# Inverting 64 unit triangles per tile: four block levels of two products each, or five doubling stages

## What is computed

```
sab = S @ kk_t
S   = S * exp(w_t) + sab (x) b_t + v_t (x) k_t
y_t = S @ r_t
```

## Time and profile before

| | |
|---|---|
| median of three runs | 6516.54 us |
| the profiled execution | 6509.57 us, span 6507.4 us |
| TensorE busy | 5869.2 us (90%) |
| VectorE busy | 3906.5 us (60%) |
| ScalarE busy | 1874.9 us (29%) |
| GpSimd busy | 937.7 us (14%) |
| mean granted TensorE clock | 0.973 |

### The profile page before, as it was taken

How to read it: one execution, slowest core, us unless ns; L and a number is a source line. 1 busy time by engine, 2 the same in 40 slices (tenths; PEclk the granted TensorE clock), 3 DMA queues, 4 the chain that set the end, 5 groups by cost and what they waited for, 6 DMA issues and landing times. The chain is left out here.

```text
span 6507.4 us, 293913 instructions
## 1 busy us (share of the span) xinstructions
PE 5869.2 (90%) x135752; PEld 4180.8 (64%) x135752; DVE 3906.5 (60%) x9323; ACT 1874.9 (29%) x3531; POOL 937.7 (14%) x900
## 2 busy tenths in 40 slices
PE   6888988998988888898888988987499999999999
PEld 5777777777777777777777777776244444444443
DVE  5777777777777777777777777775523323322300
ACT  3333333333333333333333333332000000000000
POOL 0111111111111111111111111110202202220210
PEclk9999999999999999999999999998699999999999
DMA  1000000000000000000000000000211211121120
GB/s 57 21 18 17 23 17 18 23 17 17 23 17 17 23 18 17 22 19 17 23 18 17 24 17 17 24 15 14 90 46 66 73 65 60 60 92 46 66 71 13
DMA packets 108833, 214.34 MB, mean 33 GB/s; under 512 B 25424, under 2 KB 26704, under 8 KB 107088
## 3 DMA queue, kind: packets, MB, share of 16 engines
q1 hardware_dynamic: 92240, 144.98, 7.6%
q0 software_dynamic: 15360, 50.48, 2.3%
HBM read 144.67 MB, written 50.72 MB: 30 GB/s over the span
## 5 line engine op out<-in xcount | busy, mean ns | idle before, releaser
L377 DVE COPY_PREDICATED time_raw<-time_known,w_bank 128x96 f32<-128x96 int32 (+6 forms) x3072 | 823.5, 274 | 240.3 <-PE w_bank L874 151.9
L1661 PE MATMUL moe_bank<-moe_w,moe_hidden 128*128 128x512 f32 x2048 | 928.7, 596 | 0.0
L1648 PE MATMUL moe_bank<-moe_hT,moe_w 128*128 128x512 f32 x2048 | 924.8, 594 | 0.8 <-DVE moe_hT L1548 0.8
L1648 PEld LDWEIGHTS moe_bank<-moe_hT,moe_w 128*128 128x128 f32 x2048 | 386.8, 191 | 472.3 <-issue 471.1
L1661 PEld LDWEIGHTS moe_bank<-moe_w,moe_hidden 128*128 128x128 f32 x2048 | 379.4, 190 | 429.5 <-issue 428.1
L1569 ACT ACTIVATE moe_hidden<-moe_bank,moe_b 128x512 f32<-128x512 f32 x256 | 175.9, 687 | 1628.2 <-PE moe_bank L1648 1522.9
L860 PE MATMUL w_bank<-time_invT,time_part 32*32 32x32 f32 x32768 | 418.7, 196 | 141.1 <-issue 88.2
L860 PEld LDWEIGHTS w_bank<-time_invT,time_part 32*32 32x32 f32 x32768 | 372.4, 107 | 201.3 <-issue 138.5
L849 PE MATMUL w_bank<-time_inv,time_ub 32*32 32x32 f32 x32768 | 412.6, 196 | 72.9 <-issue 38.7
L849 PEld LDWEIGHTS w_bank<-time_inv,time_ub 32*32 32x32 f32 x32768 | 355.0, 107 | 190.4 <-issue 149.9
L802 POOL TENSOR_TENSOR time_tail<-time_tail,time_lp 128x512 f32<-128x512 f32 x64 | 75.4, 1178 | 2777.8 <-ACT time_lp L732 2682.9
(11 more groups left out here) (225 smaller groups left out, 9716.9 us busy)
## 6 DMA issues: line engine op xcount, KB each, us to landing
moe_w<-in_w SPq DMA_DIRECT2D x64, 1024.0 KB, 7.2
mid_xn<-time_xn_rows SPq DMA_DIRECT2D x128, 129.0 KB, 2.7
time_x_rows<-in_x SPq DMA_DIRECT2D x128, 128.0 KB, 2.9
time_base<-in_x SPq DMA_DIRECT2D x128, 128.0 KB, 3.2
mid_acc<-time_mixed SPq DMA_DIRECT2D x128, 128.0 KB, 2.7
mid_scores<-time_rated SPq DMA_DIRECT2D x128, 2.0 KB, 1.7
moe_b<-in_b SPq DMA_DIRECT2D x8, 256.0 KB
time_receptance<-in_w_receptance SPq DMA_DIRECT2D x1, 1024.0 KB, 4.9
```

The costliest lines, as they stand in the source:

```text
L377: e.copy_predicated(by_raw[:, "uy".index(q), n0:n1, :, 0:8 * j + 8], known[:, "uy".index(q), :, :, mine].to_broadcast([P, n1 - n0, 2, 8 * ...
L1648: got = e.matmul(up[now % 3][:, :], w1[:, g * F + k * P:g * F + (k + 1) * P], hT[x % 2][:, g * CAP + half * HALF:g * CAP + (half + 1) * HA ...
L1661: got = e.matmul(down[t][:, :], hidden[now % 4][:, t * P:(t + 1) * P], tile(w2, k), start=k == 0, stop=k == FC - 1)
```

## The change

Five stages with k = 1, 2, 4, 8, 16 take the place of the four levels. `ew` holds, side by side for each unit, 32 columns E and 32 columns W. E is one factor of a Newton-like doubling and W is the inverse so far. A stage multiplies a turned factor by both (64 moving columns); the first stage needs E alone and the last needs W alone (32 columns each). Results go to both PSUM banks 6 and 7. ScalarE copies them back to `ew`, VectorE turns the E half into `grow`, and GpSimd computes `2I - grow` for the next stage. There is no `P` and `Q` pair: each stage is one run of 64 products. In the TensorE order S1, S2, S4 and S8 stand where P0, P1, P2 and P3 stood, the places of Q0, Q1 and Q2 are empty, and S16 stands where Q3 stood. GpSimd's fill with the identity and the masks `levels` are gone; GpSimd makes the first E of the next tile from `ub` (`B.e1`).

```diff
@@ on_tensor
-            def P_of(lev, half):
-                    ...
-                        e.wait_ge(dve.sem, dve[f"C.I{lev - 1}"])
-                        mm = e.matmul(BANK[f"P{lev}"][head(h), blk(n)], got["ub"][head(h), blk(n)], got["inv"][head(h), blk(n)],
-            def Q_of(lev, half):
-                    e.wait_ge(act.sem, act[f"C.P{lev}"])
-                        mm = e.matmul(BANK[f"Q{lev}"][head(h), blk(n)], part[head(h), blk(n)], got["invT"][head(h), blk(n)],
+            def inverse_stage(k, half):
+                if half == 0:
+                    clear(e, f"S{k}")
+                    clear(e, f"S{k}+")
+                    if k == 1:
++                        ...
+                        e.wait_ge(pool.old, pool.ago("B.e1"))
+                    else:
+                        e.wait_ge(pool.sem, pool[f"C.b{k // 2}"])
+                taken = {1: slice(0, N), 16: slice(N, 2 * N)}.get(k, slice(0, 2 * N))
+                by = raw_of(0) if k == 1 else grow
+                for i in range(half * HALF_U // 2, (half + 1) * HALF_U // 2):
+                    for n in (i, i + HALF_U):
+                        ...
+                            mm = e.matmul(both_banks[to, n * 2 * N + taken.start:n * 2 * N + taken.stop], by[rows, blk(n)],
+                                          got["ew"][rows, n * 2 * N + taken.start:n * 2 * N + taken.stop],
@@ on_vector
-            def invert(lev):
-                e.wait_ge(pe.sem, pe[f"C.Q{lev}"])
-                e.copy_predicated(chunks(got["invT"]), level(lev + 1, U), chunks(BANK[f"Q{lev}"])).then_inc(
-                if lev < 3:
-                    e.transpose(col(got["inv"]), col(got["invT"])).then_inc(dve.sem, dve.step(f"C.I{lev}"))
+            def turn_rest(k):
+                e.wait_ge(act.sem, act[f"C.S{k}"])
+                e.transpose(chunks(grow), rest_of(got["ew"])).then_inc(dve.sem, dve.step(f"C.t{k}"))
...
                 mask_scores("u", 4)
                 mask_scores("u", 5)
+            if Cs:
+                turn_rest(8)
...
-                e.transpose(col(out["ub"]), raw_of(0)).then_inc(dve.sem, dve.step("B.ub"))
-            if Cs:
-                invert(3)
-                e.copy_predicated(chunks(out["invT"]), level(0, U), chunks(out["ub"])).then_inc(
-                e.transpose(col(out["inv"]), col(out["invT"])).then_inc(dve.sem, dve.step("B.inv"))
+                e.transpose(sum_of(out["ew"]), chunks(raw_of(0))).then_inc(dve.sem, dve.step("B.ub"))
@@ on_scalar
+            def inverse_of(k):
+                e.wait_ge(pe.sem, pe[f"C.S{k}"])
+                if k == 1:
+                    e.copy(rest_of(got["ew"]), rest_of(both_banks)).then_inc(act.sem, act.step("C.S1"))
+                elif k == 16:
+                    e.copy(chunks(invT), sum_of(both_banks)).then_inc(act.sem, act.step("C.S16"))
+                else:
+                    e.copy(col(got["ew"]), inv_bank).then_inc(act.sem, act.step(f"C.S{k}"))
@@ on_gpsimd
-                e.tensor_copy(chunks(out["invT"]), wt["eye"][:, :].rearrange("p (o t) -> p o t", o=1).to_broadcast(
+            def grow_of(k):
+                e.wait_ge(dve.sem, dve[f"C.t{k}"])
+                e.tensor_tensor(chunks(grow), every_unit(wt["eye2"]), chunks(grow), ALU.subtract).then_inc(
...
                 queries_of("u", 0, kkn)
+            if Cs:
+                grow_of(1)
...
                 faded_of(0)
+                grow_of(2)
+                grow_of(4)
+                grow_of(8)
+                e.wait_ge(dve.sem, dve["B.ub"])
+                e.tensor_tensor(rest_of(out["ew"]), every_unit(wt["eye2"]), sum_of(out["ew"]), ALU.subtract).then_inc(
@@ on_tensor, the order around the last stage
             if Bs:
                 score("u", 4)
                 score("u", 5)
             if Cs:
-                Q_of(3, 0)
+                inverse_stage(16, 0)
             if A:
                 for name in ("mk", "aaa", "ma"):
                     ...
             if Cs:
-                Q_of(3, 1)
+                inverse_stage(16, 1)
```

More of the change, by code:

```diff
@@ L89 @@
 KEYS = 8 * (1 + 2 + 3 + 4)
+TURN = 0
+HALF_U = U // 2
+STAGES = (1, 2, 4, 8, 16)
 UNITS = [(0, 3), (3, 6), (6, 9), (9, 12), (12, 14), (14, 16)]
@@ L172, in time_mix @@
         handed = [{n: sb(f"{n}_{i}", width) for n, width in (
-            ("ub", G * P), ("inv", G * P), ("invT", G * P), ("vT", G * P), ("decay_end", U), ("shrink", U))} for i in range(2)]
+            ("ew", 2 * G * P), ("vT", G * P), ("decay_end", U), ("shrink", U))} for i in range(2)]
         for i in range(2):
@@ L180, in time_mix @@
         yTs = [sb(f"yT{i}") for i in range(2)]
-        part, rhs, corr = sb("part"), sb("rhs", SU * N), sb("corr", SU * N)
+        grow, invT, rhs, corr = sb("grow"), sb("invT"), sb("rhs", SU * N), sb("corr", SU * N)
         state, faded, grown = sb("state", SU * N), sb("faded", SU * N), sb("grown", SU * N)
@@ L256, in time_mix @@
         ACT_STEPS = (
-            "A.carried A.x B.ek3 C.P0 A.mix B.ek012 D.squares B.eq D.lnv N.lnv D.rstd N.rstd B.v C.P1 A.hid_g A.hid_w A.hid_a "
-            "D.affine0 D.affine1 D.affine2 D.affine3 A.hid_kkk A.hid_mk C.P2 A.exp_z A.tail A.k C.P3 A.tna A.tnma "
-            "A.thmk A.sq N.xn B.e0 B.decay_end B.shrink C.u0 A.lp A.lns N.ln2 A.rs N.rs2 C.y0 C.u1 A.decayed A.r C.y1").split()
+            "A.carried A.x B.ek3 C.S1 A.mix B.ek012 D.squares B.eq D.lnv N.lnv D.rstd N.rstd B.v C.S2 A.hid_g A.hid_w A.hid_a "
+            "D.affine0 D.affine1 D.affine2 D.affine3 A.hid_kkk A.hid_mk C.S4 A.exp_z A.tail A.k C.S8 A.tna A.tnma "
+            "A.thmk C.S16 A.sq N.xn B.e0 B.decay_end B.shrink C.u0 A.lp A.lns N.ln2 A.rs N.rs2 C.y0 C.u1 A.decayed A.r C.y1").split()
         POOL_STEPS = (
-            "B.rk B.eye B.qu B.qy C.faded0 A.lt B.us C.faded1 B.ys").split()
+            "B.rk B.qu C.b1 B.qy C.faded0 C.b2 C.b4 C.b8 B.e1 A.lt B.us C.faded1 B.ys").split()
         PE_STEPS = (
-            "A.x D.centre C.P0 A.mix A.scored C.Q0 D.var A.delta D.gate B.value C.P1 B.bonus A.gate1 A.low_wa A.delta3 B.u0 C.Q1 "
-            "B.u1 A.low_k C.P2 B.u2 C.Q2 A.key B.u3 A.decay C.P3 B.u4 B.u5 A.low2 C.Q3 B.y0 B.y1 A.sums C.z0 B.y2 "
+            "A.x D.centre C.S1 A.mix A.scored D.var A.delta D.gate B.value C.S2 B.bonus A.gate1 A.low_wa A.delta3 B.u0 "
+            "B.u1 A.low_k C.S4 B.u2 A.key B.u3 A.decay C.S8 B.u4 B.u5 A.low2 C.S16 B.y0 B.y1 A.sums C.z0 B.y2 "
             "B.y3 C.u0 C.y0 D.out B.y5 B.y4 C.z1 C.u1 A.recept C.y1").split()
@@ L459, in on_vector @@
             if Cs:
-                invert(0)
+                turn_rest(1)
             if A:
@@ L845, in P_of @@
                     else:
-                        e.wait_ge(dve.sem, dve[f"C.I{lev - 1}"])
-                for n in range(half * U // 2, (half + 1) * U // 2):
-                    for h in range(HG):
-                        mm = e.matmul(BANK[f"P{lev}"][head(h), blk(n)], got["ub"][head(h), blk(n)], got["inv"][head(h), blk(n)],
-                                      start=True, stop=True, skip_group_check=True)
-                if half:
-                    mm.then_inc(pe.sem, pe.step(f"C.P{lev}"))
@@ L854, in Q_of @@
-            def Q_of(lev, half):
-                if half == 0:
-                    clear(e, f"Q{lev}")
-                    e.wait_ge(act.sem, act[f"C.P{lev}"])
-                for n in range(half * U // 2, (half + 1) * U // 2):
-                    for h in range(HG):
-                        mm = e.matmul(BANK[f"Q{lev}"][head(h), blk(n)], part[head(h), blk(n)], got["invT"][head(h), blk(n)],
-                                      start=True, stop=True, skip_group_check=True)
-                if half:
-                    mm.then_inc(pe.sem, pe.step(f"C.Q{lev}"))
+                        e.wait_ge(pool.sem, pool[f"C.b{k // 2}"])
@@ new lines, in inverse_stage @@
+                taken = {1: slice(0, N), 16: slice(N, 2 * N)}.get(k, slice(0, 2 * N))
+                by = raw_of(0) if k == 1 else grow
+                for i in range(half * HALF_U // 2, (half + 1) * HALF_U // 2):
+                    for n in (i, i + HALF_U):
+                        turned_in = TURN * (n // HALF_U) * (k in (4, 16))
+                        turned_out = TURN * (n // HALF_U) * (k in (2, 8))
+                        for h in range(HG):
+                            rows, to = head((h + turned_in) % HG), head((h + turned_out) % HG)
+                            mm = e.matmul(both_banks[to, n * 2 * N + taken.start:n * 2 * N + taken.stop], by[rows, blk(n)],
+                                          got["ew"][rows, n * 2 * N + taken.start:n * 2 * N + taken.stop],
+                                          start=True, stop=True, skip_group_check=True)
@@ L1171, in time_mix_inputs @@
     t = row % N
-    same = lambda size: t // size == i // size
-    upper = {h: same(2 * h) & (t // h == i // h - 1) for h in (1, 2, 4, 8, 16)}
     f32 = lambda a: np.ascontiguousarray(a.astype(np.float32))
@@ L1199, in time_mix_inputs @@
```

(1 more changed line is left out.)

100 lines of the change are left out of this document (43 added, 57 removed), and 8 rows, old and new, of the table DVE_STEPS.

## The result

The changed kernel takes 6733.8 us (median of four runs, 6726.7 to 6740.1), against 6517.0 for the kernel before (median of four runs beside it): a ratio of 1.034 (95% interval 1.032 to 1.036), 217 us slower. The forecast was 6595 us with a range of 6430 to 6680, so the direction was right and the size lies outside the range.

What follows compares the result with a forecast made beforehand. TensorE was taken to set the pace at 69.8 us a turn; 68.9 us of path plus 2.3 of low clock gave 71.2, +1.4 a turn over some 62 turns, +85 us: 6595 us, range 6430 to 6680.

Steps and rivals of the forecast that it cites:

- the path's sum: Eight links through one turn, stalls included: 68.9 us a turn at full clock without issue gaps.
- the issue gaps: TensorE waits the profile does not explain, 1.9 us a turn before two lines; forecast to be gone after the change.
- the five stalls: TensorE waits before `var` 1.5, u1 2.0, S4 1.2, S8 0.6 and S16 4.0 us; 9.3 us in sum.
- case D: Rival: issue gaps stay, clock falls at three places; 73.9 us a turn at worst, half the excess 6680 us; chance 0.13.
- link 4: Path from u2 through masked copies, transpose, hop, subtraction, hop to S8 at 2033.9; TensorE stalls 0.6 us.
- The clock's term: Lower TensorE clock behind stalls: 1.6 stretches a turn at 1.43 us, 2.3 us; mean clock about 0.96.
- A: Rival: same path, but stalls do not lower the clock; turn 68.9 to 69.2 us, about 6460 us; chance 0.16.
- B: Rival: stalls shorter than added up, most saved work arrives; at best 67.6 us a turn, 6375 us; chance 0.10.
- C: Rival: stalls come, clock stays as in the kernel before; 70.1 us a turn, 6530 us; chance 0.15.
- the 2.0 us of work: TensorE half runs fall from 10.9 to 8.9 us a turn; forecast that the stalls eat this saving.

Runs made afterwards that it cites:

- v4: Changed kernel with stages, VectorE turns and ScalarE copies reordered, no product added or left out: 6248.3 us, 0.961 of the kernel before.
- The control: Kernel before, four levels and products untouched, with `gate` behind delta3 and the squares and copy of P0 first on ScalarE: 6481.0 us, ratio 0.992.

## Why the prediction was wrong

*Right.* The direction; the work on TensorE (16 half runs to 10, 1.03 us for 64 columns); every link of the path from the start of the turn to S4 within 0.35 us; S16 5.1 us behind u4 (4.94); and that the clock falls where the stalls are. What the forecast named as tests came out so: 3.7, 1.0, 1.8 and 1.4 us of stall before S16, S4, u1 and `var` where 4, 1.2, 2 and 1.5 were forecast, and the waits on issue down from 3.4 to 0.8 us a turn. The exception is the size of the clock's fall: 0.92 where 0.96 was forecast.

*The step that failed is the end of the path's sum*: "what is won is that the issue gaps have gone, because fewer instructions pass in each microsecond and every stall lets the fetch run ahead". With the clock kept up, the turn should then take 68.9 us. The kernel with four of the five stalls filled has the clock up (0.99) and takes 71.2 us, 2.0 us of it on issue (83.8 us in 42.1 turns): 69.2 us without, 0.3 above the sum. That 0.3 is `gate`'s wait for ScalarE's reading of the variance (11.8 us in 42.1 turns), which I had not listed. So with the clock up the missing 2.3 us a turn are 2.0 of issue gaps and 0.3 of path. The gaps had been 3.4 us a turn over all lines, of which the forecast read 1.9 from two; 1.4 went, and the sum had let all of them go. The forecast itself had said that the turn would be about 1.5 us longer by the other reading, and put this into case D at half its size. D in full, 73.9 us, was nearest to what came (73.4).

One small slip in the sum: the terms of link 4 add up to 2034.05 for S8 and not 2033.9, the last hop being left out.

*The clock's term was too small as well, if one reads the changed kernel by itself.* There the gaps were 0.8 us a turn and the path 0.3, so that 3.4 of the 4.5 us above 68.9 are left for the clock, where 2.3 were forecast. The traced turn agrees: it takes 71.96 us, 3.1 above the sum. From S4 to its second half it needs 3.68 us in place of 2.11 (S4's first half and `low_k` at full clock, 1.03 and 1.08), and from S16 to `from_values` 5.90 us in place of 4.15, of which 0.17 are on issue. That is 1.6 us of low clock at each of the two places, against 1.43 forecast for one stretch, and the average turn is 1.4 us longer still. The two readings of the excess differ because the low clock and the issue gaps seem to stand in for each other; the runs do not part them further.

*Net of the gaps the clock's term was right in its sum and wrong in its parts.* From 73.4 to 71.2 us the clock is worth 2.2 us a turn net, where 2.3 were forecast. But 11.7 us a turn ran at the lower level and not 5.5. I had counted 1.6 stretches of the length seen in the earlier trace rows; the low level lasted longer behind the long stalls, as in the 6.80 us window above. A microsecond of it cost less than in the earlier trace rows (2.2 us for some 10 that the fills took away, against 1.43 for 3.4), I think because behind S16 it took the place of issue gaps. That I was right there is luck.

*Rivals.* A fell, with a mean clock of 0.92 in the loop. B fell: the five stalls are 8.4 us in the traced turn and 8.1 on average, against 9.3 added up. C fell with the clock.

*Where the 2.0 us of work went.* Into five stalls of 8 us in sum, for want of cover. v4 speaks for it: with the same products in an order that covers the new links, the turn is 4.2 us shorter than before, 7.8 shorter than in the changed kernel. The control takes part of that back: some of the order helps the four levels too.

## What to carry to other kernels

Fewer products do not help if each now stands behind a longer chain of engines: write down for each link what the waiting engine will do meanwhile, and move the links (here the transposes on VectorE and a copy on ScalarE) ahead of waits that they don't need. The price of a stall of TensorE is not its length. It is the length, less the issue gaps that it swallows, and more for the low clock behind it: put into the kernel before, a stall of 2.4 us cost 1.8 us a turn, and 0.5 of that came back when it was filled; in the changed kernel, with 8 us of stalls, 2.2 us a turn came back. Take the gaps from all lines of the waits and do not put them at nothing: here a stall left 2.2 of 3.4 us a turn.

## What the runs showed of the hardware that was not expected

Issue gaps came 106 records behind a filled 4 us stall, and where the clock rose they returned (79.8 us in 41.1 turns at a clock of 0.96, against 30.9 in 40.9 at 0.92). Many of them lie a fixed number of records apart: in the kernel before, from 2000 to 2240 us, 10 of the 18 distances between two such waits are 125 to 127 records, and each record has a weight load beside it. That speaks for something that happens once in a fixed number of instructions. The Trainium skill (Runtime: NRT & Kernel Launch, Instruction fetch mechanics) says that fetch is mostly hidden; if these gaps are fetches, the measured 2.0 us a turn differs. Their cause was not tested and stays open. And work that fills stalls and is thrown away made the kernel 134 us faster.
